# An attention and expert kernel: routing in smaller and earlier steps, gates and results finished pair by pair, one slot copy

## The reference

```python
x = L0_attn_inputs                     # (8, 512, 128)
xn = layernorm(x)
s = attention(xn, W_qkv, W_out)        # 32 query heads, 16 key/value heads of 64, causal, ALiBi
g = silu(experts(xn, gate_w, gate_b, w1, b1, w2, b2))   # 8 experts, the best 2 of each token,
x = x + s * g                          # softmax of the two gate values, 128 -> 512 (exact GELU) -> 128
```

## Time and profile before

| | |
|---|---|
| three timed runs | 1232.81, 1232.95, 1229.16 us; median 1232.81 |
| profiled execution, its own time | 1230.63 us |
| its span | 1228.8 us |
| PE, DVE busy | 1128.3 us (92%), 994.0 us (81%) |
| ACT, POOL busy | 927.5 us (75%), 873.5 us (71%) |
| mean granted TensorE clock | 0.968 of full speed |

### The profile page before, as it was taken

One profiled execution on the slowest core, in us unless ns is written; L12 is line 12 of the kernel. 1 busy time (PEld: TensorE's weight loads), 2 busy tenths in 40 slices (PEclk: granted clock), 3 DMA queues, 4 the chain that ended last, 5 costly groups with the idle time before them and its releaser, 6 DMA issues. The chain is left out here.

```text
span 1228.8 us, 51239 instructions
## 1 busy us (share of the span) xinstructions
PE 1128.3 (92%) x16970; PEld 832.7 (68%) x16970; DVE 994.0 (81%) x3099; ACT 927.5 (75%) x1808; POOL 873.5 (71%) x1082
## 2 busy tenths in 40 slices
PE   2578999999999999998998889999999999999994
PEld 1355776676777777776887656777777777777773
DVE  8768888888888888884777767888888888888875
ACT  3356888888888888886666567888888888888883
POOL 8036899999998888885000057888888888888886
PEclk8579999999999999999999989999999999999997
DMA  8324666655566555565434255655555555555554
GB/s 264 142 56 87 131 132 132 138 128 126 138 126 130 128 127 128 128 133 92 88 88 113 65 136 120 125 122 119 119 119 119 119 119 119 119 119 119 119 121 95
DMA packets 267759, 148.89 MB, mean 121 GB/s; under 512 B 172946, under 2 KB 256242, under 8 KB 266996
## 3 DMA queue, kind: packets, MB, share of 16 engines
q1 hardware_dynamic: 263540, 138.85, 50.9%
q0 software_dynamic: 4096, 8.40, 2.4%
HBM read 15.76 MB, written 16.78 MB: 26 GB/s over the span
## 5 line engine op out<-in xcount | busy, mean ns | idle before, releaser
L792 POOL TENSOR_TENSOR t_lo<-stage 128x512 f16<-128x512 f32 x640 | 654.4, 1038 | 174.8 <-ACT stage L1198 172.0
L1462 DVE CUSTOM_DVE_ANT_0 stage<-ps,kmask 128x512 bf16<-128x512 f32 (+3 forms) x1024 | 451.7, 488 | 108.5 <-PE ps L891 83.7
L1198 ACT ACTIVATE stage<-ps,slope 128x512 f32<-128x512 f32 (+1 forms) x768 | 440.0, 618 | 96.0 <-PE ps L928 83.5
L919 PE MATMUL ps<-q_st,k_st 128*128 128x256 f16 (+3 forms) x1024 | 300.7, 303 | 12.7 <-issue 5.4
L951 PE MATMUL outs<-v_sp,stage 128*128 128x65 f16 x2560 | 263.9, 195 | 7.1 <-POOL t_lo L792 6.5
L953 PE MATMUL outs<-v_sp,stage 128*128 128x64 f16 x2560 | 262.7, 194 | 0.0
L955 PE MATMUL outs<-v_sp,t_lo 128*128 128x65 f16 x2560 | 262.7, 194 | 0.0
L951 PEld LDWEIGHTS outs<-v_sp,stage 128*128 128x128 bf16 x2560 | 235.8, 98 | 29.9 <-issue 14.6
L953 PEld LDWEIGHTS outs<-v_sp,stage 128*128 128x128 bf16 x2560 | 236.0, 99 | 0.0
L955 PEld LDWEIGHTS outs<-v_sp,t_lo 128*128 128x128 f16 x2560 | 235.7, 98 | 0.0
L920 PE MATMUL ps<-q_st,k_st 128*128 128x128 f16 x1024 | 224.2, 219 | 0.0
(11 more groups left out here) (205 smaller groups left out, 2665.9 us busy)
## 6 DMA issues: line engine op xcount, KB each, us to landing
q_st<-stage SPq DMA_DIRECT2D x256, 128.0 KB, 2.4
k_st<-stage SPq DMA_DIRECT2D x128, 128.0 KB
q_st<-stage SPq DMA_DIRECT2D x256, 64.0 KB, 2.1
k_st<-stage SPq DMA_DIRECT2D x128, 64.0 KB
slot_y<-stage SPq DMA_DIRECT2D x40, 128.0 KB, 2.0
X<-in_L_attn_inputs SPq DMA_DIRECT2D x8, 512.0 KB, 8.5
slot_x<-att SPq DMA_DIRECT2D x2, 2048.0 KB, 8.7
wx_raw<-in_L_ffn_w SPq DMA_DIRECT2D x64, 64.0 KB
```

Of the source, the lines that this page charges most:

```text
L792: pool.tensor_tensor(t_lo[r], t_p[r], upper(t_p[r]), ALU.subtract).then_inc(s[f"lo{u % NG}"], 1)
L919: pe.matmul(d, k[:, 0, at], q[:, 0, seen], start=(c0 == 0), stop=False, skip_group_check=True)
L1198: e = act.activation(t_p[r][:, c0:c1], S_ps[u % 2][:, c0:c1], ACT.Exp, scale=slope[:, bass.ds(pair_index(n) * 2 * SLOTS + sl * 2 + h, 1)])
L1462: ins = dve.tensor_tensor_reduce(junk[h][:, c0:c0 + w], M_ps[h][:, c0:c0 + w], kmask[:, SEQ - w:SEQ], -1.0 / 1024, 3e38, ALU.add, ALU.min, ...
```

## The change

- Before the first half: the gate products of a batch follow the turning of the batch four later. The output weights' low part is made by GpSimd in four pieces, and the bias rows by GpSimd in five, behind L tasks of bodies 0 and 1 (`in_between`).
- Routing: `choose` in six steps in body 0, `route` in nine, the slot steps ahead of the weights and of the block numbers; the rank products behind C0 of body 0.
- Rows go with bodies 2 to 30, a second one with 4, 7 and 10; weights one window earlier. So the last window of the half has neither. The written part of the first half is 12 windows, the loop 16, and 4 more.
- One copy brings both slot numbers of a tile.
- The GELU table is loaded ahead of the half's last `out_hi` copy; `project` of body 30 stands between the first hidden products and the first block.
- Second half: the gate is z times (0.5 tanh(z/2) + 0.5), made for pairs of tiles: ACT (T) makes the hyperbolic tangent and the affine step, GpSimd (U) the product of `mix` with `att`, that with the gate, and the sum with X, and SP (H) writes the pair. So 28 tiles are finished inside the bodies. The last four tiles are finished by all engines at the end, the last accumulation going straight into the result in two halves.

```diff
@@ order, first half: ("W0", 0, ..) becomes ("W0", 1, ..) on ACT, POOL and SP; POOL loses ("I1", 1, 64)
@@ order, second half
 ACT:  ("K0", 2, 38), +("T0", -3, 38), ("E4", 0, 42)
 POOL: ("L0", 0, 10), +("U2", -4, 10), ("L1", 0, 18), ("G0", -1, 25), ("L2", 0, 27), +("U0", -3, 27),
       ("I0", 1, 41), ("L4", 0, 47), -("I1", 1, 54), ("L5", 0, 56), +("U1", -3, 56), ("L6", 0, 63)
 SP:   ("A1", -1, 60), +("H0", -4, 60), ("Q1", 1, 76)
...
-        FIRST_ONES = {"DVE": [("B1", 0), ("B3", 0), ("B5", 0), ("B3", 1), ("B5", 1), ("N0", 0), ("B3", 2), ("B5", 2),
-                              ("N0", 1), ("B3", 3), ("B5", 3)],
-                      "PE": [("V0", 1)], "ACT": [("E4", 0)]}
-        CHOICES = 3
+        FIRST_ONES = {"DVE": [("B1", 0), ("B3", 0), ("B5", 0), ("B7", 0), ("B9", 0), ("B11", 0),
+                              ("B3", 1), ("B5", 1), ("B7", 1), ("B9", 1), ("N0", 0), ("B11", 1),
+                              ("N0", 4), ("N0", 6), ("N0", 8)],
+                      "PE": [("C0", 0)], "ACT": [("C1", 0)],
+                      "POOL": [("L1", 0), ("L3", 0), ("L5", 0), ("L7", 0), ("L9", 0), ("L1", 1), ("L4", 1), ("L6", 1), ("L9", 1)]}
+        CHOICES = 6
...
-            start, end = lo + (max(TWICE) + UNROLL if lo == 0 else 2 * UNROLL), hi - UNROLL
+            start, end = lo + (max(TWICE) + UNROLL if lo == 0 else 2 * UNROLL), hi - (2 * UNROLL if lo == 0 else UNROLL)
...
+        FIRST_SENT, TWICE = 2, (4, 7, 10)
+        SENDERS = range(FIRST_SENT, FIRST_SENT + NT - len(TWICE))
...
+            def hand_out(n, par, _):
+                if par == 1 and finishes(n):
+                    t, pairs = pair_of(n, par)
+                    sp.wait_ge(s["fin"], pairs)
+                    sp.nop(nofuse=True)
+                    sp.dma_start(ot[:, bass.ds(t, 2), :], X[:, bass.ds(t, 2), :]).then_inc(s["outd"], 16)
...
+            def in_between(k):
+                if k < O_STEPS:
+                    c = slice(k * HKV * D // O_STEPS, (k + 1) * HKV * D // O_STEPS)
+                    hi, lo = (w[:, :, :].rearrange("p j d -> p (j d)")[:, c] for w in (wo_hi, wo_lo))
+                    pool.wait_ge(s["wo_hi"], 1)
+                    pool.tensor_tensor(lo, wo_in[:, c], hi, ALU.subtract).then_inc(s["wo_lo"], 1)
+                    return
...
+            def indices(t, at):
+                pool.tensor_copy(slot_now[at][:, :].unsqueeze(2), slot_of[:, :, bass.ds(t, 1)]).then_inc(s["ready"], 1)
...
+            def finish(n, par, k):
+                if par == 0 or not finishes(n):
+                    return
+                t, pairs = pair_of(n, par)
+                m = tiles_of(mix, t)
+                if k == 0:
+                    pool.wait_ge(s["tangent"], pairs)
+                    pool.wait_ge(s["acc"], n)
+                    pool.nop(nofuse=True)
+                    pool.tensor_tensor(m, m, tiles_of(att, t), ALU.mult).then_inc(s["summed"], 1)
+                elif k == 1:
+                    pool.wait_ge(s["summed"], pairs)
+                    pool.wait_ge(s["sigmoid"], pairs)
+                    pool.nop(nofuse=True)
+                    pool.tensor_tensor(m, m, g_pair, ALU.mult).then_inc(s["gated"], 1)
+                else:
+                    pool.wait_ge(s["gated"], pairs)
+                    pool.wait_ge(s["xend"], 64)
+                    pool.nop(nofuse=True)
+                    pool.tensor_tensor(tiles_of(X, t), tiles_of(X, t), m, ALU.add).then_inc(s["fin"], 1)
...
+            def gate_products(q):
+                pe.wait_ge(s["xlo"], q + 1)
+                for t in range(q * QT, (q + 1) * QT):
+                    gate_product(t)
...
                 hidden(0, 0, expert_of(0), g)
+            for n in LATE_O[:-1]:
+                project(n, n % UNROLL, 0)
             for sl in range(SLOTS):
                 pe.wait_ge(s[f"al{sl}"], HALF)
             for c in range(STEP):
                 for g in range(PARTS):
                     step_of(0, c, g)
-                for n in {0: LATE_O[:-1], 2: LATE_O[-1:]}.get(c, ()):
+                for n in {2: LATE_O[-1:]}.get(c, ()):
...
-            def gates(c):
-                g = out_chunk(mix, c)
-                act.activation(g, g, ACT.Silu).then_inc(s["silu"], 1)
+            def gates(n, par, _):
+                if finishes(n):
+                    t, pairs = pair_of(n, par)
+                    if par == 0:
+                        act.wait_ge(s["added"], t + 2)
+                        need(act, "gated", pairs - 1)
+                        act.nop(nofuse=True)
+                        act.activation(g_pair, tiles_of(mix, t), ACT.Tanh, scale=0.5).then_inc(s["tangent"], 1)
+                    else:
+                        act.wait_ge(s["tangent"], pairs)
+                        act.activation(g_pair, g_pair, ACT.Identity, bias=half[:, 0:1], scale=0.5).then_inc(s["sigmoid"], 1)
             def out_hi(n, _, sl):
-                final = isinstance(n, int) and (n, sl) == (BODIES - 1, 1)
-                if final:
-                    act.wait_ge(s["added"], NT)
-                    for c in range(2):
-                        gates(c)
+                if isinstance(n, int) and (n, sl) == (HALF - 1, 1):
+                    act.preload_act_table(ACT.Gelu)
...
-            split_hi(O_PART)
+            act.wait_ge(s["wo"], 16)
+            act.activation(wo_hi[:, :, :].rearrange("p j d -> p (j d)"), wo_in, ACT.Copy, scale=WS)
+            act.activation(wo_in, wo_in, ACT.Copy, scale=WS).then_inc(s["wo_hi"], 1)
...
+            act.wait_ge(s["added"], NT)
+            act.activation(g_last[:, :], tiles_of(mix, LAST, QT), ACT.Tanh, scale=0.5).then_inc(s["tangent"], 1)
+            act.wait_ge(s["tangent"], LAST // 2 + 1)
+            act.activation(g_last[:, :], g_last[:, :], ACT.Identity, bias=half[:, 0:1], scale=0.5).then_inc(s["sigmoid"], 1)
+            act.wait_ge(s["fin_last"], 2)
+            act.dma_start(ot[:, LAST + QT // 2:NT, :], X[:, LAST + QT // 2:NT, :]).then_inc(s["outd"], 16)
...
+            leave_bodies("DVE", tasks, HALF, BODIES, late=[BODIES - 1])
+            dve.wait_ge(s["gated"], LAST // 2 + 1)
+            dve.wait_ge(s["acc"], BODIES - 1)
+            dve.wait_ge(s["xend"], 64)
+            xx, a, m = (tiles_of(v, LAST, QT) for v in (X, att, mix))
+            dve.tensor_tensor(a, a, m, ALU.mult).then_inc(s["partial"], 1)
+            dve.wait_ge(s["partial"], 1)
+            dve.tensor_tensor(xx, xx, a, ALU.add).then_inc(s["partial"], 1)
+            dve.wait_ge(s["partial"], 2)
+            dve.wait_ge(s["op"], BODIES)
+            for c in range(2):
+                cols = slice(c * SEQ // 2, (c + 1) * SEQ // 2)
+                dve.scalar_tensor_tensor(out=a[:, cols], in0=bank_of("O0")[:, cols], scalar=1.0 / WS, in1=m[:, cols],
+                                         op0=ALU.mult, op1=ALU.mult).then_inc(s["fresh"], 1)
+                dve.wait_ge(s["fresh"], c + 1)
+                dve.tensor_tensor(xx[:, cols], xx[:, cols], a[:, cols], ALU.add).then_inc(s["fin_last"], 1)
```

More of the change, by code:

```diff
@@ L175, in build @@
         ones = sb("ones", [P, P], F16)
+        half = sb("half", [P, 1], F32)
         NSTG, CH = 3, 2048
@@ L206, in build @@
         xg_more = sb("xg_more", [P, LOAD * BT * 2 * P], F16)
-        slot_now = [[sb(f"slot_now{k}{at}", [P, 1], U32) for at in range(3)] for k in range(2)]
+        slot_now = [sb(f"slot_now{at}", [P, 2], U32) for at in range(3)]
         y_now = [[sb(f"y_now{k}{par}", [P, D], F32) for par in range(2)] for k in range(2)]
@@ L271, in build @@
         names = """x0 x1 x2 x3 wq0 wq1 wo sm ident consts small
-            stat rstd norm xnD xnA xtr xhi xlo b1tr b1 gate gate_w whi wlo attz var topexp gap silu
-            picked ranked kept routed zeros ready0 ready1 rhi sent0 sent1 sent2 got00 got01 got10 got11 weighed0 weighed1 added
+            stat rstd norm xnD xnA xtr xhi xlo b1tr b1 gate gate_w whi wlo wo_hi wo_lo numbered attz var topexp gap
+            picked ranked kept routed zeros ready rhi sent0 sent1 sent2 got00 got01 got10 got11 weighed0 weighed1 added
             w_in w_hi w_lo xend
             xload0 xload1 hmm0 hmm1 gelu0 gelu1 hhi hlo0 hlo1 ymm yout ystore0 ystore1
-            gated0 gated1 gated2 rd0 rd1 nrm0 nrm1 op acc ta0 ta1 ah0 ah1 al0 al1 rows
+            tangent sigmoid summed gated partial fresh rd0 rd1 nrm0 nrm1 op acc ta0 ta1 ah0 ah1 al0 al1 rows
             turnc crow0 crow1 copied
@@ L522, in build @@
         ROW_STEPS = 3 + 2 + 5 + 2 * 4
+        ot = out.rearrange("b (t p) d -> p (b t) d", p=P)
         @block.sync
@@ L621, in _ @@
             for at in range(UNROLL):
-                sp.wait_ge(s[f"sent{at}"], (HALF - FIRST_SENT) // UNROLL * 32)
+                sp.wait_ge(s[f"sent{at}"], len([n for n in SENDERS if n % UNROLL == at]) * 32)
             sp.wait_ge(s[f"sent{UNROLL}"], len(TWICE) * 32)
@@ L701, in _ @@
             pool.memset(b2_row[:, :, :], 0.0).then_inc(s["consts"], 1)
+            pool.memset(half[:, :], 0.5)
```

(16 more changed lines are left out.)

225 lines of the change are left out of this document (105 added, 120 removed), and 4 rows, old and new, of the table ORDER.

## The result

The changed kernel takes 1219.81 us (median of 4 runs, 1216.96 to 1220.89), the kernel before 1232.88 (4 runs): 13.1 us less, a ratio of 0.9894 (95% interval 0.987 to 0.9918). The forecast was 1209 with a range of 1202 to 1218: the sign is right, the gain is little more than half of it, and the time lies above the range. The profiled execution has a span of 1218.7 us, 10.1 us under the span before, and a time of 1220.46.

What follows compares the result with a forecast made beforehand. TensorE's work was taken to bound the steady first half, with losses at the start, last body, switch and tail. Terms -11.8 - 0.2 - 1.6 - 1.3 + 1.0 - 9.4 = -23.3 us took 1232.81 to about 1209, range 1202 to 1218.

Steps and rivals of the forecast that it cites:

- Up to the first turn: Stretch to body 0's shift counts: earlier gate products and smaller selection batches save 4.3 us, bounds -3.0 and -5.0.
- Body 0: First body: the wait that goes, the ranks and added slot steps nearly cancel; -0.7 us, bounds -3.5 and +2.
- I keep -11.8, since part of it is in the durations above: Start through body 2: saves 11.8 us, with 5.2 us of possible loss from VectorE and GpSimd excluding each other left out.
- In return VectorE's 4.14 wait goes: Body 0: VectorE's 4.14 us wait for the copy of the rank counts disappears.
- The term for the ranks: Just after body 0's turn: 33 rank products and their copy put 1.1 us on the path to body 1's first rough product.
- Bodies 1 and 2: TensorE's idling behind VectorE's slot steps goes, half the bias pieces' time counts against it; -4.8 and -2.0 us.
- Bodies 3 to 30: Rest of first half: fewer double sends and slot copies against more looped bodies and postponed routing; -0.2 us, bounds ±1.5.
- VectorE has 1.9 us free: +0.5: Bodies 4, 6 and 8: postponed routing steps fall where VectorE has 1.9 us free, costing 0.5 us.
- Second half: Its 26 steady bodies: pair work on ScalarE and GpSimd, less a slot copy per body; +1.0 us, bounds 0 and +5.
- Tail: End of the kernel: no SiLU ahead of the copy, shorter last operations and a smaller store; -9.4 us, bounds -8 and -10.5.
- 2.0 to landing and some 0.5 of end: Tail: after the last VectorE operation, a 128 KB store and the end replace 5.3 us from last add to end.
- rival of a weak start: Start: VectorE's chain through body 0 stays as long and bodies 1 and 2 inherit it; -4, so 1217 us; chance 0.08.

Runs made afterwards that it cites:

- sixth version: Changed kernel with GpSimd's low parts of body 0 subtracted over 16 of 512 columns, the rest left out as zero; 1217.75 us.
- tenth run: Seventh run with the output weights' pieces moved to body 1 and the rank products behind the first scores of body 0; 1213.57 us.
- the first: Changed kernel with GpSimd's nine extra pieces (output weights and bias rows) done ahead of the first body; 1221.25 us.
- seventh run: Changed kernel with bias rows made ahead of the first half and the three postponed routing batches behind VectorE's accumulation O0; 1213.40 us.
- eighth version: Changed kernel with the two last stores carrying 16 of 128 partitions each, most of the last four tiles left out; 1218.25 us, one run.
- fourth run: The kernel before, unchanged, run again for a second trace; 1236.21 us.

## Why the prediction was right and wrong

*Up to the first turn* (-4.3 forecast, -5.5 measured): right, but just beyond its bounds, for a reason that it didn't have. Smaller routing steps do fill VectorE's gaps: it idles for 2.4 of 15.8 us there instead of 4.7 of 20.7. The rest is GpSimd holding VectorE up again: with the bias rows gone from GpSimd, the product of 28 columns takes 0.19 us instead of 1.45 in the kernel before. Without these 1.3 us it would be about -4.2.

*Body 0* (-0.7, +3.8): here the prediction failed, in two of its steps. The larger is "I keep -11.8, since part of it is in the durations above". It counted the shared port once, by durations read where the same steps had met GpSimd only now and then. In the changed body all of them stand beside low parts and weights' pieces: eight took 0.59 to 1.28 us, and those of them that some trace shows without such a wait take 0.17 to 0.42 there. VectorE is busy for 6.2 us more than before, where 3.1 was forecast: 3.0 of the 4.5 us by which body 0 missed. With the low parts cut short it is 3.4 more (sixth version). The 5.2 us that the paragraph on that rule gave as the price, and the sum left out, was thus too high, but much nearer than nothing. The second step is "In return VectorE's 4.14 wait goes". A wait of 5.12 us behind the rank products took its place, and VectorE's idle time fell by 2.3 us where 3.8 was forecast, which is the other 1.5. The Trainium skill, page "SBUF — State Buffer", section "Who interferes with whom", also says that a tensor_scalar in a fast two-port form shares the lock, and that the loser waits for the whole instruction; the 1.05 against 0.22 for the comparison agrees, and 4.42 us for one operation beside a run of seven goes beyond it. The term for the ranks (1.1) was too small for the same reason: the group of 32 products took 3.75 us at a granted clock of 0.50, the level of 1.2 GHz, behind 15.80 us in which TensorE was busy for 6.48, against 2.0 at the full clock; but where they stand made no measurable difference (tenth run).

*Bodies 1 and 2* (-4.8 and -2.0; -3.9 and +2.0): TensorE's waits behind VectorE's slot steps went as forecast. The bias pieces were priced as half their duration on the path; they are moved ahead of the first sends in GpSimd's queue, the row copies wait for the sends' landing and the low parts stand behind them. They cost 4.3 us in body 2 alone, shown by the first and the seventh run.

*Bodies 3 to 30* (-0.2, +5.8): "VectorE has 1.9 us free: +0.5" took free time for a free port. Batches of three steps behind N0 met the end of a long GpSimd run, and in the changed kernel's trace body 4 is 2.2 us longer, body 6 0.8 and body 8 0.5 than in the seventh version's. The double sends themselves cost 1.3 to 1.6 each in the seventh version, near the forecast. The rest is a low clock: bodies 7 and 10 of the changed kernel's trace ran at 0.90 and 0.91 and took 16.63 and 18.47 us; in the eighth version, which has the same code there, they ran at the full clock and took 15.56 and 16.60, and bodies 3 to 30 took 433.7 us, 3.5 less. The prediction had no term for it, and its cause wasn't tested: waits of TensorE of 1.98 us (body 6) and of 0.97 and 0.46 us (body 10) stand just ahead of it, but no low clock followed the wait of 1.98 in body 4.

*Last body and switch* (-2.9, -2.1): right in mechanism. The table load stands at 570.05, under ScalarE's wait, and the wait for the first GELU is gone.

*Second half* (+1.0, +1.4 and an unforecast -5.2): +1.4 is -1.9 for one slot copy and +3.2 for U1, each missing from the working in that size. The start of the half was mostly a difference between executions (fourth run). GpSimd didn't become the bound, and no table is loaded in the loop: 651 ScalarE instructions instead of 625 in the 26 bodies are the two for each of 13 pairs and nothing else. The Trainium skill, page "ScalarE: Activation LUTs", section "Table sets: the hidden batching unit", has tanh and exp in one set; the trace agrees.

*Tail* (-9.4, -6.3): right down to the last add, 7.2 us after the normalisation ended (1206.56 to 1213.78; forecast 7.7). Wrong by the term "2.0 to landing and some 0.5 of end": 4.9 us lie between the last add and the end of the span, and smaller stores don't shorten them (eighth run). Another 1.1 us of the miss lie ahead of it, in the last two bodies up to the end of the normalisation (30.69 us instead of 29.61), with no reason shown.

The forecast's rival of a weak start (-4 instead of -11.8) was nearer to what happened: up to body 3 the start gave -3.6. Its mechanism was partly another: VectorE's chain through body 0 became longer, and body 2 was held up by GpSimd's queue.

## What to carry to other kernels

Idle time of an engine is not room for a step: look at what GpSimd does at that very time. A small VectorE step beside a run of GpSimd subtractions can last as long as the rest of the run, and the same step beside GpSimd's DMA issues took 0.4 us; so try a place for each step and read its duration, not the busy share. Read the other side too when work leaves an engine: the bias rows cost 4.3 us where they went and gave back 1.3 where they had been. When a step waits for another's result, look at what will stand ahead of that result in its new place. Work moved in GpSimd's queue ahead of a send costs what waits for the send. At the end of a kernel, look for which queue closes last before making the last store smaller.

## What the runs showed of the hardware

- One VectorE tensor_scalar on 128x32 took 0.43, 1.36 or 4.42 us by what GpSimd did beside it; the long ones ended with GpSimd's run of seven 1.04 us subtractions. In body 0 similar steps waited for one piece only (1.05 us for the comparison beside a piece that ended at 64.92). What decides between one piece and the run was not tried.
- A step on 8 columns (L1501, 0.97 us against 0.17) lost 0.80 us, and one on 256 (L1508, 1.28 against 0.42) 0.86: in these cases the loss did not grow with the size of the step.
- A GpSimd subtraction on a single partition holds VectorE up as well: a product of 128x28 took 1.45 to 1.48 us beside one and 0.19 without it, each time until the subtraction's end.
- GpSimd's bias pieces on one partition of 1024 elements took 1.03 to 2.12 us each, the shorter ones as long as a low part of 128 partitions by 512 (1.04).
- From TensorE's last product to the end of the span pass 6.1 us in most traces and up to 6.75 in others; with 16 KB in each of the last two stores instead of 128 it is 6.1 too.
